# Expert stage of a mixture-of-experts layer: 23 blocks of 512 slots become 16 of 512 and 7 of 256

## The reference, cut to what matters

```python
x = x + attention(layernorm(x))
h = layernorm(x).reshape(T, 512)
probs = softmax(h @ gate_w.T);  topk_w, topk_ids = top_k(probs, 2)
gates[token, topk_ids] = topk_w / sum(topk_w)          # zero elsewhere
routed = sum_e gates[:, e] * ((silu(h @ w_gate[e]) * (h @ w_up[e])) @ w_down[e])
shared = (silu(h @ sw_gate) * (h @ sw_up)) @ sw_down
x = x + routed + shared
```

## Time and profile before

| | before |
|---|---|
| median of 3 runs | 2493.39 us |
| the profiled execution | 2498.08 us, span 2496.3 us, mean granted clock 0.967 |
| busy: PE, DVE, ACT, POOL | 2293.5, 1517.2, 1042.4, 1196.7 us |
| shared stage, from the trace | about 1474 to 1857 us |
| expert stage, from the trace | about 1857 to 2496 us |

### The profile page before, as it was taken

One profiled execution on the slowest core, in us unless ns is written; L12 is line 12 of the kernel. 1 busy time (PEld: TensorE's weight loads), 2 busy tenths in 40 slices (PEclk: granted clock), 3 DMA queues, 4 the chain that ended last, 5 costly groups with the idle time before them and its releaser, 6 DMA issues. The chain is left out here.

```text
span 2496.3 us, 32769 instructions
## 1 busy us (share of the span) xinstructions
PE 2293.5 (92%) x11973; PEld 1440.7 (58%) x11973; DVE 1517.2 (61%) x3302; ACT 1042.4 (42%) x1925; POOL 1196.7 (48%) x763
## 2 busy tenths in 40 slices
PE   6997599999999999999999968999969999999997
PEld 5775344444444444444444336777758788788786
DVE  4664687767777676777767435565545555555553
ACT  3332055555555555555555542122123333333432
POOL 0100046555675655567565674545443444544543
PEclk9999599999999999999999989999989999999999
DMA  5666611314032131423212114343245656566661
GB/s 167 252 252 224 129 35 35 85 35 98 22 71 66 41 85 29 117 60 70 67 38 64 29 40 146 102 135 119 85 153 193 198 185 200 185 197 197 186 156 34
DMA packets 171616, 286.07 MB, mean 115 GB/s; under 512 B 30137, under 2 KB 72633, under 8 KB 171456
## 3 DMA queue, kind: packets, MB, share of 16 engines
q1 hardware_dynamic: 145152, 210.45, 28.8%
q0 software_dynamic: 26304, 73.54, 9.9%
HBM read 198.61 MB, written 92.38 MB: 117 GB/s over the span
## 5 line engine op out<-in xcount | busy, mean ns | idle before, releaser
L880 ACT ACTIVATE b_pt<-b_st 128x512 f32<-128x512 f32 (+3 forms) x1280 | 612.8, 535 | 492.0 <-DVE b_st L842 206.8
L697 POOL TENSOR_TENSOR b_acc<-b_acc,b_pt 128x1024 f32<-128x1024 f32 (+1 forms) x256 | 592.8, 2346 | 215.6 <-ACT b_pt L880 215.3
L821 DVE TENSOR_REDUCE b_mpart<-b_mx 128x1 f32<-128x512 f32 x768 | 511.9, 686 | 200.6 <-PE b_mx L937 198.0
L958 PE MATMUL b_st<-b_q,b_k 97*128 97x512 f32 (+2 forms) x1280 | 497.5, 401 | 75.9 <-ACT b_pt L880 54.5
L937 PE MATMUL b_mx<-b_k,b_q 96*128 96x512 f32 (+2 forms) x1280 | 508.5, 412 | 27.0 <-DVE b_mt L829 23.0
L937 PEld LDWEIGHTS b_mx<-b_k,b_q 96*128 96x128 f32 x1280 | 248.0, 195 | 283.9 <-DVE b_mpart L821 156.4
L958 PEld LDWEIGHTS b_st<-b_q,b_k 97*128 97x128 f32 x1280 | 242.4, 191 | 281.4 <-ACT b_pt L880 240.3
L971 PE MATMUL b_ob<-b_pt,b_v 128*32 128x512 f32 (+3 forms) x2560 | 304.3, 548 | 1.1 <-ACT b_pt L880 1.1
L818 DVE CUSTOM_DVE_ANT_0 b_unread<-b_mx,b_later 128x384 bf16<-128x384 f32 (+3 forms) x512 | 244.6, 484 | 90.3 <-PE b_mx L937 90.0
L697 POOL TENSOR_TENSOR b_acc<-b_pt 128x1024 f32<-128x1024 f32 x48 | 113.4, 2378 | 300.9 <-ACT b_pt L880 300.9
L69 PE MATMUL e_fb<-e_xh,e_w_guh 128*128 128x512 f32 (+1 forms) x552 | 220.5, 400 | 1.5 <-DVE e_xl L1782 1.5
(11 more groups left out here) (223 smaller groups left out, 3516.0 us busy)
## 6 DMA issues: line engine op xcount, KB each, us to landing
b_q<-scr_qh SPq DMA_DIRECT2D x64, 256.0 KB, 4.5
b_k<-scr_kh SPq DMA_DIRECT2D x64, 256.0 KB, 4.0
sw_gu<-in_L_ffn_w_gate_dram SPq DMA_DIRECT2D x12, 704.0 KB, 4.4
sw_gu<-in_L_ffn_w_up_dram SPq DMA_DIRECT2D x12, 704.0 KB, 5.8
a_xin<-in_L_attn_x_dram POOLq DMA_DIRECT2D x8, 1024.0 KB, 5.7
scr_qh<-a_qh SPq DMA_DIRECT2D x8, 1024.0 KB, 4.9
scr_ql<-a_ql SPq DMA_DIRECT2D x8, 1024.0 KB, 7.0
scr_kh<-a_kh SPq DMA_DIRECT2D x8, 1024.0 KB, 4.4
```

What stands on the lines that cost most here:

```text
L697: g.tensor_tensor(out[:, :, lo:], so_far[:, :, lo:], pt[n % NPB][:, :, lo:], ALU.add).then_inc(s_add, 1)
L821: v.tensor_reduce(part, mxb[i % NMX][:, 0:w], AX.X, ALU.max).then_inc(s_red, 1)
L880: act.activation(pt[n % NPB][:, j, lo:], stb[:, (2 * n + j) % NST, lo:], ACT.Exp, scale=SCALE).then_inc(s_exp, 1)
L958: pe.matmul(stb[:, (2 * n + j) % NST, lo:], kb[:, h, at:at + P], qb[:, h, q * CH + lo:(q + 1) * CH], start=True, stop=True).then_inc(s_st, 1)
```

## The change: what it does, and the diff

A unit is 256 slots, a pair 512. Each expert's tokens are cut into pairs, with one single unit at the end where 256 or fewer are left over; 39 units are the most that can be needed. They are laid into 16 blocks of 512 slots (`WHOLES`) and 7 of 256 (`HALVES`); `map_blocks` finds each block's expert and first place in 20 DVE instructions, from 10 more constants that POOL makes. `SPOT[b]` is b.

In a block of 256, everything that runs over tokens takes 256 columns or 2 tiles; its weights are fetched and split as before. Down tiles of a short block go to banks 2 and 3, so that the next block's first two products wait for none of them. In all blocks POOL scatters each tile when it is ready. In the last block the first down tile is finished ahead of the second.

In the shared stage, `choose` is cut in three and put between the tiles of the next chunk's `residual`; the first chunk's multiplication goes from POOL to DVE, and POOL's first additions wait for DVE's `o_low`.

```diff
+UNITS = (2 * T + E * (UNIT - 1)) // UNIT
+WHOLES = 2 * T // SLOTS
+HALVES = UNITS - 2 * WHOLES
+NB = WHOLES + HALVES
+TILES = [4 if b < WHOLES else 2 for b in range(NB)]
+ABOVE = [sum(TILES[:b]) for b in range(NB + 1)]
@@ POOL, shared stage @@
 def normalize(c, first=False):
     if not first:
         g.wait_ge(s_o, c * 80)
-    g.tensor_tensor(on[:], oin[:], rin[:], ALU.mult).then_inc(s_on, 1)
+        g.tensor_tensor(on[:], oin[:], rin[:], ALU.mult).then_inc(s_on, 1)
     g.wait_ge(s_x, c * 16 + 16)
     g.wait_ge(s_on, c + 1)
+    if first:
+        g.wait_ge(s_ol, 1)
@@ DVE, shared stage, residual, in its loop over tiles t @@
     v.bn_stats(st[:, t], x1[:, t]).then_inc(s_stat, 1)
+    if not first and t < 2:
+        choose(c - 1, t)
+    if not first and t == 2:
+        count_choices(c - 1)
@@ DVE, the first instruction of the shared stage @@
+v.tensor_tensor(on[:], oin[:], rin[:], ALU.mult).then_inc(s_on, 1)
 v.wait_ge(s_wh, 1)
 v.tensor_tensor(wol[:], wos[:], f32(woh[:]), ALU.subtract).then_inc(s_wl, 1)
@@ DVE, map_blocks, the wide instructions: [P, 23, 8] becomes [P, 23, 16] @@
+    wide = [P, NB, NG]
+    then(v.tensor_tensor(ended[:], spot[:].unsqueeze(2).to_broadcast(wide), endg[:].unsqueeze(1).to_broadcast(wide), ALU.is_ge))
+    then(v.tensor_tensor(ended_by[:], ended[:], turn[:].unsqueeze(1).to_broadcast(wide), ALU.mult))
+    then(v.tensor_reduce(ebf[:], ended_by[:], AX.X, ALU.add))
@@ POOL, expert stage @@
 def scatter(b):
-    g.wait_ge(s_y, b * TPB + TPB)
-    for t in range(TPB):
+    for t in range(TILES[b]):
+        g.wait_ge(s_y, ABOVE[b] + t + 1)
@@ ACT, expert stage, as one of the instructions over tokens @@
-act.activation(sg[0:width, f], fb[2 * f][0:width, :], ACT.Silu).then_inc(s_sg, 1)
+act.activation(sg[0:width, f, cols(b)], fb[2 * f][0:width, cols(b)], ACT.Silu).then_inc(s_sg, 1)
@@ PE, expert stage @@
-            if j < TPB and not first:
-                pe.wait_ge(s_y, (b - 1) * TPB + j + 1)
-            gate_up(nc, fb[j][:], wt[n], which, f, xh[n], xl[n]).then_inc(s_gu, 1)
+            if not first and TPB - TILES[b - 1] <= j < TPB:
+                pe.wait_ge(s_y, ABOVE[b] - TPB + j + 1)
+            gate_up(nc, fb[j][:, cols(b)], wt[n], which, f, xh[n][:, :, cols(b)], xl[n][:, :, cols(b)]).then_inc(s_gu, 1)
...
     pe.wait_ge(s_hl, b * NF + NF - 1)
-    for t in range(TPB):
-        down(nc, fb[t][:], wt[n], hh, hl, t, range(NF - 1))
+    ahead_of_last = range(TILES[b] // 2) if last else range(TILES[b])
+    for t in ahead_of_last:
+        down(nc, down_bank(b, t)[:], wt[n], hh, hl, t, range(NF - 1))
     pe.wait_ge(s_hl, b * NF + NF)
-    for t in range(TPB):
-        down(nc, fb[t][:], wt[n], hh, hl, t, [NF - 1]).then_inc(s_dn, 1)
+    for t in range(TILES[b]):
+        if t not in ahead_of_last:
+            down(nc, down_bank(b, t)[:], wt[n], hh, hl, t, range(NF - 1))
+        down(nc, down_bank(b, t)[:], wt[n], hh, hl, t, [NF - 1]).then_inc(s_dn, 1)
```

More of the change, by code:

```diff
@@ L32 @@
 SLOTS = 512
-NB = (2 * T + E * (SLOTS - 1)) // SLOTS
+UNIT = SLOTS // 2
+UNITS = (2 * T + E * (UNIT - 1)) // UNIT
+WHOLES = 2 * T // SLOTS
+HALVES = UNITS - 2 * WHOLES
+NB = WHOLES + HALVES
 TPB = SLOTS // P
+TILES = [4 if b < WHOLES else 2 for b in range(NB)]
+ABOVE = [sum(TILES[:b]) for b in range(NB + 1)]
+SPOT = [TILES[:b].count(TPB) if TILES[b] == TPB else WHOLES + TILES[:b].count(TPB // 2) for b in range(NB)]
 PLACES = E * T + NB * SLOTS
@@ L1122, in phase_shared @@
         pads = al.sb("c_pads", [P, RUN, 3], U32)
[L1123 to L1128, removed]
+        NG = 2 * E
+        starts = al.sb("c_starts", [P, 2, E, T // SLOTS])
+        spot = al.sb("c_spot", [P, NB])
+        lone, paired, second = al.sb("c_lone", [P, HALVES + 1]), al.sb("c_paired", [P, HALVES + 1]), al.sb("c_second", [P, HALVES + 1])
+        leap, turn = al.sb("c_leap", [P, NG]), al.sb("c_turn", [P, NG])
+        below, ng, endg = al.sb("c_below", [P, 2, E, T // SLOTS]), al.sb("c_ng", [P, 2, E]), al.sb("c_endg", [P, NG])
+        step_g, pairs, offs = al.sb("c_step_g", [P, NG]), al.sb("c_pairs", [P, 1]), al.sb("c_offs", [P, HALVES])
+        ended, ended_by = al.sb("c_ended", [P, NB, NG]), al.sb("c_ended_by", [P, NB, NG])
+        ebf, rowf = al.sb("c_ebf", [P, NB]), al.sb("c_rowf", [P, NB])
+        scan_ones = al.sb("c_scan_ones", [P, NG])
         ab = [al.bank(f"c_ab{n}") for n in range(2)]
@@ L1432, in _ @@
                 v.reciprocal(rsum[:], sums[:]).then_inc(s_rs, 1)
[L1434 to L1458, removed]
-                    v.tensor_tensor(gap[:], m[1][:], m[0][:], ALU.subtract).then_inc(s_gap, 1)
-                    with nc.allow_low_precision(reason="counts of at most 32 in bf16"):
-                        then(v.tensor_tensor(both[:], oh2[:, 0], oh2[:, 1], ALU.add))
-                        for t in range(TPC - 1):
-                            then(v.tensor_tensor(sooner[c % 2][:, t + 1], sooner[c % 2][:, t], both[:, t], ALU.add))
-                        v.tensor_tensor(sooner[1 - c % 2][:, 0], sooner[c % 2][:, TPC - 1], both[:, TPC - 1], ALU.add).then_inc(s_both, 1)
                 def slots(c):
@@ L1479, in map_blocks @@
                     v.wait_ge(s_cnt, 1)
-                    wide = [P, NB, E]
-                    then(v.tensor_tensor(below[:], starts[:], lb[:, CNT:CNT + E].unsqueeze(2).to_broadcast([P, E, T // SLOTS]), ALU.is_lt))
-                    then(v.tensor_reduce(nb[:], below[:], AX.X, ALU.add))
-                    then(v.tensor_tensor_scan(endb[:], scan_ones[:], nb[:], 0.0, ALU.mult, ALU.add))
-                    then(v.tensor_tensor(ended[:], blk[:], endb[:].unsqueeze(1).to_broadcast(wide), ALU.is_ge))
@@ L1490, in map_blocks @@
-                    then(v.tensor_copy(keep["place"][:], rowf[:]))
-                    then(v.tensor_scalar(ebf[:], ebf[:], float(E - 1), None, ALU.min))
-                    v.tensor_copy(keep["expert"][:], ebf[:]).then_inc(s_map, 1)
+                    wide = [P, NB, NG]
+                    counts = lb[:, CNT:CNT + E].unsqueeze(1).unsqueeze(3).to_broadcast([P, 2, E, T // SLOTS])
+                    then(v.tensor_tensor(below[:], starts[:], counts, ALU.is_lt))
+                    then(v.tensor_reduce(ng[:], below[:], AX.X, ALU.add))
@@ L1497, in step @@
                         token_rows(c)
-                        choose(c)
+                        for n in range(2):
+                            choose(c, n)
+                        count_choices(c)
                         hidden(c, 0)
@@ L1695, in turns, with tile_turns, cols, down_bank @@
             return b // 2 + 1
+        def tile_turns(b):
+            return sum(TILES[b % 2:b + 1:2])
+        def cols(b):
+            return slice(0, TILES[b] * P)
+        def down_bank(b, t):
+            return fb[t if TILES[b] == TPB else TPB - TILES[b] + t]
         with nc.Block() as block:
```

108 lines of the change are left out of this document (77 added, 31 removed).

## The result

The changed kernel took 2407.58 us (median of 4 runs, 2398.04 to 2411.99) and the kernel before, beside it on the same chip, 2494.47 (2489.29 to 2498.41): a ratio of 0.9644 [0.9626, 0.9663]. The forecast was 2405 us, 88.6 us less; 86.9 came off. The profiled executions are 2498.08 and 2403.58 us, 94.5 apart. In five later rounds the changed kernel had 2404.27 us and a ratio of 0.9624 [0.9599, 0.9649].

What follows compares the result with a forecast made beforehand. PE bounds both stages now; short blocks would be bound by ACT's and DVE's order. Gains 80.3 (expert stage) + 7.7 + 1.0 - 0.4 = 88.6 us off the median 2493.39 give 2404.8 us; 8-in-10 range 2388 to 2424.

Steps and rivals of the forecast that it cites:

- The short block, 16.0 us: Expert stage: a 256-slot block takes 16.0 us, set by ACT's and DVE's order of work with the next weights' split.
- PE alone 13.7 us; 0.12 for 256 columns: Short block: PE's own work sums to 13.7 us, with 256-column matmuls starting 0.12 us apart.
- the rival in which the matmuls do not halve: Short blocks: at 0.18 us a matmul PE needs 18.0 us a block, program 2421 us; chance 0.13.
- an estimate by it was 12.8: Short block: PE's sum would be 12.8 us if weight loads of 107 ns set the matmul pace.
- POOL and DMA each have 5 us or more before they are late.: Short blocks: if the cover goes, row and weight transfers still have 5 us or more of slack.
- some 2 us for the scatter's landing: POOL's queue: the gather waits some 2 us for the scatter to land, part of 10.5 us a short block.
- The rival's large fall: Short blocks: PE's clock falls from 2.4 to 1.2 GHz, about 26 us a block, program about 2475; chance 0.06.
- The tail, 3.9 us: Program's end: scatter by tile cuts the time from PE's end to the last scatter's end from 6.9 to 3.0 us.
- The shared stage, 7.7 us: Shared stage: `choose` behind the first tiles removes 7 of 8 PE waits of 1.1 us, gaining 7.7 us.
- One sign failed: Shared stage: PE's wait of `c_ab` for `c_x` (from `residual`) was to shrink to under 1 us in all.
- The start, 1.0 us: Shared stage's start: the first multiplication on DVE, taking turns with POOL's additions, gains 1.0 us, up to 3 side by side.
- `map_blocks`: Before the expert stage: 20 DVE instructions instead of 12, about 3 us more, costing 0.4 us, at worst 3.

Runs made afterwards that it cites:

- no_low_split: Changed kernel, but for blocks 17 to 22 DVE subtracts only 8 columns of each weight part's low parts; short block 13.55 us, expert stage 7.7 us shorter.
- early_split: Changed kernel, but in short blocks ACT and DVE split the next block's weights before the work on h; 2393.61 us.
- early_small: Changed kernel with weight splits ahead of h in short blocks and about 1% of the weight bytes for blocks 18 to 22; short blocks 14.18 or 14.19 us.
- small_weights: Changed kernel, but blocks 18 to 22 fetch about 1% of their weight bytes; blocks stay at 15.8 us, one at 17.2.
- scatter_all: Changed kernel, but POOL's scatter again waits for all tiles of a block before the first one; 2406.11 us.
- undo_shared: Changed kernel with its two shared-stage edits taken back (choose before residual, first multiplication on POOL); 2414.96 us, ratio 0.9691 to the kernel before.
- early_interleaved: Changed kernel with short blocks between whole ones and weight splits ahead of h in short blocks; 2393.32 us, ratio 0.9589; in five later rounds 2389.29, 0.9579.
- interleaved: Changed kernel with the same blocks in another order, each short one between or behind whole ones; 2401.86 us, ratio 0.9626 to the kernel before.
- x_first: Changed kernel, but POOL gathers the rows of x before waiting for the scatter to land; expert stage 544.5 us, 6.4 longer.

## Why the prediction was right, and where it was not

- **The short block, 16.0 us.** Right, with its cause: 15.8 in five of six. The half-width durations came from rows, and walking through the block in the given order found what the sums of ACT and DVE (8 and 11 us) could not. That the order holds it is shown from both sides: no_low_split (13.55) and early_split with early_small (14.19). Its waits are listed with 1.23 us for the last split (1.40 from start to start) and 0.4 for the low part of h, where 1.5 and 0.7 were forecast.
- **PE alone 13.7 us; 0.12 for 256 columns.** Right: 13.55, and starts 0.12 apart. That rules out the rival in which the matmuls do not halve. The Trainium skill, TensorE: Matmul & The Clock Gate, LDWEIGHTS, gives a weight load as its columns over 1.2 GHz, and an estimate by it was 12.8; the 13.55 lies nearer to the trace's pace.
- **"POOL and DMA each have 5 us or more before they are late."** Wrong. The gather's wait of "some 2 us for the scatter's landing" was taken from rows of whole blocks; in a short one the weights' transfers (9.9 us to landing, forecast 6.6) fill most of the block, and the landing takes 4.5 us and at most 6.6 (1.7 without their bytes, small_weights). It cost 1.6 us in one block here, and four times 1 to 2.7 us once the order was out of the way (no_low_split). The prediction priced the landing from stretches with less traffic beside it. None of the 16.0 us rested on it, so the forecast time hardly suffered.
- **The clock.** The rival's large fall did not come (its 26 us a block was itself low: PE's 13.7 doubled are 27.4). A small one did: 1.4 to 1.5 us in one short block of six, and up to 3 us in the first chunk of the shared stage. The forecast had no term for it.
- **The tail, 3.9 us.** To the last scatter's end it gave 3.91 us, by the steps named. Another 3.97 us came behind it: the span ended 8.05 us after the fourth scatter in a row and ends 4.1 us after the last of two. The prediction took the part behind the last issue as fixed, so that half of the gain was not foreseen. It is not the distance between the scatters: scatter_all's two, 0.3 us apart, also leave 4.0. That it is the bytes queued there is my reading and was not tested apart.
- **The shared stage, 7.7 us.** The mechanism was right (undo_shared), the term mis-sized: 11.1 over seven chunks. Chunks are 1.39 us closer (43.06 and 41.67), where the list had 1.1: a listed wait starts at the matmul's recorded end and leaves out the refill. That makes 9.7 of the 11.1. The rest is luck: in two chunks before and one after, DVE's low part of h starts beside POOL's multiplication, takes 5.1 us in place of 0.69, and costs 1.2; undo_shared had that once, and the changed kernel in another chunk the next time. One sign failed: the wait for `residual` was to shrink to under 1 us in all, and is 1.9 in the first chunk (0.4 before), since PE's first tile there now starts 3.4 us closer to the stage's start and `residual` only 1.8.
- **The start, 1.0 us.** 1.8: three operations at 2.29 us and not 2.4, and 9.7 for the joint part and not 10.0. That DVE and POOL take turns was the right model: DVE's 2048 columns took 4.87 us beside POOL and take 2.29 with POOL still. The Trainium skill, SBUF — State Buffer, SBUF: two separate sides, calls the port pair of VectorE and GpSimd an exclusive lock, held for a whole instruction. The trace agrees, also in DVE's operation over 32 columns that took 1.17 us beside POOL's additions.
- **`map_blocks`.** 20 operations (five of them of double width, not four) and 6.2 us against 3.3, as forecast 3 us more; the way from the last chunk's mark to the first silu grew by 0.7 us, forecast 0.4.

## What to carry to other kernels

When the body of a loop shrinks but part of its work (here the split of weights) does not, walk the new body in program order on every engine: the period was 15.8 us with no engine busy above 14.2, and moving the fixed work ahead of the work that waits made it 14.2. Price a DMA's landing from a stretch with the same traffic beside it: the same scatter was waited for 1.7 us without weights in flight and up to 6.6 with them. And read a stall from start to start, since the listed wait was 0.2 to 0.3 us short of the time lost.

## What was unexpected of the hardware

- In the nine profiles in which PE waits 1 us or more in most short blocks, 14 of the 54 short blocks had a granted clock of 0.90 to 0.92 and, where no row was late as well, took 1.4 to 1.7 us longer; which ones changed from execution to execution. In the three executions in which PE waited at most 0.4 us at a time there (early_interleaved twice, early_small) none of 18 did. So short stops of PE seem to cost more than themselves, by chance: some 6 us in interleaved. A long stop is not enough for it: no_low_split, with waits of up to 2.4 us, had no such block. The first chunk of the shared stage, with its long waits, shows the same at 28 or 31 us. What exactly sets it off the runs don't show.
- In whole blocks POOL waits 2.2 us for the landing when scatters leave after the whole block and 4.6 when they leave tile by tile, with the same bytes.
- Asking earlier is not safe: x_first removed all of PE's waits for rows, and its expert stage was 6.4 us longer, 3.9 of them in whole blocks at full clock.
